# Moving the keys' sine products from GpSimd to VectorE in the first attention layer

## The reference, cut to what matters

```python
def _rotate_half(x):
    half = x.shape[-1] // 2
    return jnp.concatenate([-x[..., half:], x[..., :half]], axis=-1)
...
kv_r = kv_c * cos + _rotate_half(kv_c) * sin
scores = jnp.einsum('bhsr,bhlr->bhsl', q_r, k_r)
attn = jax.nn.softmax(scores, axis=-1)
ctx_c = jnp.einsum('bhsl,bld->bhsd', attn, kv_r)
```

## Time and profile before

| | |
|---|---|
| device time, median of 3 runs | 3006.91 us (3006.22 to 3009.59) |
| device time of the profiled execution | 3003.31 us |
| its span | 3001.5 us |
| mean granted TensorE clock | 0.958 |
| TensorE busy (matmul) | 2737.8 us, 91% |
| VectorE busy | 1884.5 us, 63% |
| ScalarE busy | 1130.2 us, 38% |
| GpSimd busy | 1837.4 us, 61% |

### The profile page before, as it was taken

One profiled execution on the slowest core, in us unless ns is written; L12 is line 12 of the kernel. 1 busy time (PEld: TensorE's weight loads), 2 busy tenths in 40 slices (PEclk: granted clock), 3 DMA queues, 4 the chain that ended last, 5 costly groups with the idle time before them and its releaser, 6 DMA issues. The chain is left out here.

```text
span 3001.5 us, 43374 instructions
## 1 busy us (share of the span) xinstructions
PE 2737.8 (91%) x16024; PEld 1697.7 (57%) x16024; DVE 1884.5 (63%) x2324; ACT 1130.2 (38%) x1641; POOL 1837.4 (61%) x1233
## 2 busy tenths in 40 slices
PE   7689999999999998998789979999999999997998
PEld 6445554555555454554678865555555555555665
DVE  3486666665766576663666656765765765675664
ACT  2124441444134432443333224443443443442331
POOL 0369985999669975994200008877877877950111
PEclk8689999999999999998899989999999999998998
DMA  9323341333213431333000042332333323301000
GB/s 302 107 75 94 78 117 32 76 89 93 70 46 93 100 88 32 80 83 110 1 1 1 1 86 65 88 80 67 87 72 74 84 66 81 89 9 49 7 7 13
DMA packets 98842, 209.21 MB, mean 70 GB/s; under 512 B 30306, under 2 KB 74322, under 8 KB 91116
## 3 DMA queue, kind: packets, MB, share of 16 engines
q1 hardware_dynamic: 98636, 206.44, 26.8%
HBM read 135.36 MB, written 46.00 MB: 60 GB/s over the span
## 5 line engine op out<-in xcount | busy, mean ns | idle before, releaser
L1423 DVE TENSOR_REDUCE maxpart<-pair 112x2 f32<-112x1000 f32 x748 | 896.2, 1198 | 461.8 <-PE pair L1055 460.1
L1242 ACT ACTIVATE prob<-wide 125x896 f32<-125x896 f32 x768 | 675.0, 917 | 809.1 <-PE wide L1081 556.6
L1309 POOL TENSOR_TENSOR sums<-sums,prob 125x448 f32<-125x448 f32 x544 | 675.7, 1263 | 47.8 <-POOL sums L1309 39.3
L1312 POOL TENSOR_TENSOR sums<-sums,prob 125x896 f32<-125x896 f32 x284 | 615.0, 2166 | 117.5 <-ACT prob L1242 81.2
L1095 PE MATMUL single<-prob,kv 125*64 125x448 f32 x3072 | 672.0, 551 | 0.7 <-ACT prob L1242 0.7
L1076 PE MATMUL wide<-qhigh,kparts 64*125 64x448 f32 x3072 | 451.4, 371 | 14.0 <-ACT prob L1242 12.4
L1055 PE MATMUL pair<-kparts,qhigh 64*112 64x500 f32 x1496 | 337.1, 446 | 61.4 <-DVE maxpart L1423 53.5
L1095 PEld LDWEIGHTS single<-prob,kv 125*64 125x64 f32 x3072 | 211.5, 136 | 253.4 <-issue 190.4
L1055 PEld LDWEIGHTS pair<-kparts,qhigh 64*112 64x112 f32 x1496 | 131.0, 171 | 361.8 <-DVE maxpart L1423 190.3
L1076 PEld LDWEIGHTS wide<-qhigh,kparts 64*125 64x125 f32 x3072 | 282.1, 184 | 84.8 <-issue 30.4
L1081 PE MATMUL wide<-shift,ones_row 64*125 64x448 f32 x1536 | 283.9, 364 | 0.2 <-DMA shift<-maxrow 0.2
(11 more groups left out here) (406 smaller groups left out, 4034.4 us busy)
## 6 DMA issues: line engine op xcount, KB each, us to landing
kparts<-keys_merged SPq DMA_DIRECT2D x64, 750.0 KB, 8.9
kparts<-kparts SPq DMA_DIRECT2D x96, 250.0 KB, 3.1
keys_merged<-kparts SPq DMA_DIRECT2D x32, 750.0 KB, 10.4
recip<-zrec_merged SPq DMA_DIRECT2D x124, 112.0 KB, 2.8
w_low_values<-w_merged SPq DMA_DIRECT2D x64, 192.0 KB, 2.8
raw<-in_ctx SPq DMA_DIRECT2D x32, 375.0 KB
values_merged<-kv SPq DMA_DIRECT2D x32, 375.0 KB
kv<-values_merged SPq DMA_DIRECT2D x32, 375.0 KB
```

The source lines that it names most:

```text
L1242: nc.scalar.activation(prob[:, n_ % NPROB, :].rearrange("p (a b) -> p a b", a=2), acc[0:LP, :, 0:HQ], ACT.Exp)\
L1309: nc.gpsimd.tensor_tensor(dst[:, cols], first_in[:, cols], prob[:, n_ % NPROB, cols], ALU.add)\
L1312: nc.gpsimd.tensor_tensor(dst, first_in, prob[:, n_ % NPROB, :], ALU.add).then_inc(s["pool_sum"], 1)
L1423: V.tensor_reduce(maxpart[:, b % 2, t:NMAX:4, third], acc[0:TQ, :, 0:LB], AX.X, ALU.max).then_inc(*R.signal_drained(kind, *key))
```

## The change

From batch 3 on, the step `rotate` on GpSimd is gone from the list. In its place VectorE has two steps `sine`, one for each half of the features, with the same operands, shape and count of `rope_sin`. While batch `b` is at pair 2 the first is issued for batch `b + 3`; at pair 4 the second, followed by the first half of the cosine products, which stood at pair 3; the second half of the cosine products, which stood at pair 4, moves to pair 0 of the next batch. `rope` stays at pair 1. Batches 0 to 2 keep their rotation on GpSimd. All products read `raw` and a table and write to SBUF.

```diff
@@ -310,8 +310,6 @@
                 ahead(t + 1)
                 if j + 1 < BG and p == 4:
                     add("maxT", b + 1, region=3)
-                if p == 3 and b + 3 < NB:
-                    add("rotate", b + 3)
                 if p in (2, 3) and b + 2 < NB:
                     add("keyT", b + 2, p - 2, region=3)
                 if p == 5 and j < BG - 1 and b + 2 < NB:
@@ -329,8 +327,13 @@
                     if b + 2 < NB:
                         add("rope", b + 2, 0)
                         add("rope", b + 2, 1)
-                if p in (3, 4) and b + 3 < NB:
-                    add("ropecos", b + 3, p - 3)
+                if p == 2 and b + 3 < NB:
+                    add("sine", b + 3, 0)
+                if p == 4 and b + 3 < NB:
+                    add("sine", b + 3, 1)
+                    add("ropecos", b + 3, 0)
+                if p == 0 and 1 <= b and b + 2 < NB:
+                    add("ropecos", b + 2, 1)
                 if p == 4 and j == BG - 1 and b + 2 < NB:
                     add("keyT", b + 2, 2, region=3)
                 if p == 5 and b + 2 < NB:
@@ -1336,6 +1339,12 @@
                         dve.wait_ge(s["tables_loaded"], 32)
                     dve.wait_ge(s[f"ctx_loaded_{b % 2}"], 16 * (b // 2 + 1))
                     V.tensor_tensor(rope_c[:, tiles, :], raw[:, b % 2, tiles, :], cosk[:, tiles, :], ALU.mult).then_inc(s["rope_cos"], 1)
+                elif kind == "sine":
+                    b, part = key
+                    dve.wait_ge(s["rope_done"], 2 * b)
+                    dve.wait_ge(s[f"ctx_loaded_{b % 2}"], 16 * (b // 2 + 1))
+                    own, other = (slice(0, DC // 2), slice(DC // 2, DC))[::1 - 2 * part]
+                    V.tensor_tensor(rope_s[:, :, own], raw[:, b % 2, :, other], sink[:, :, own], ALU.mult).then_inc(s["rope_sin"], 1)
                 elif kind == "rope":
                     b, part = key
                     tiles = slice(part * LT // 2, (part + 1) * LT // 2)
```

## The result

| | before | changed |
|---|---|---|
| device time, median of 4 runs | 3006.56 us | 2963.40 us (2962.20 to 2970.34) |
| ratio, with its 95% interval | | 0.9862 [0.9846, 0.9877] |
| profiled execution: device time, span | 3003.31, 3001.5 us | 2962.20, 2960.4 us |

The kernel became faster by 1.4%, 43 us in the medians and 41.1 in the profiled spans.

What follows compares the result with a forecast made beforehand. GpSimd was taken to pace the first layer's full stretches. Removal 1.75 us less, added product costs 1.0 more: 0.75 less a stretch; 14.3 and 1.2 make 15.5 off 3006.9, so 2991.4 us, range 2974 to 3012.

Steps and rivals of the forecast that it cites:

- GpSimd paces the full stretch, TensorE's floor is 26.65: First layer: GpSimd's work sets the 29.70 us between context copies; TensorE's limit allows at most 3.05 us gain.
- The removal, 1.75 us a stretch: Two sine products leave GpSimd at pair 3: 1.92 us out, a 0.17 us wait in, 1.75 us less.
- VectorE has room, and the context rows come in time: VectorE, 18.88 of 29.70 us busy, takes 1.1 more; context rows, wanted 1.4 us earlier, add nothing.
- (1) The first sine product at 298.5 is 0.76 into the pair of 297.74: 0.76 + 0.55 - 0.12 = 1.2: At pair 2, VectorE's first sine product lengthens GpSimd's pair of half sums by 1.2 us.
- The rule behind it: A VectorE product costs GpSimd its own length, plus how far into a half sum it starts, less 0.12 us.
- (2) ... 1.55: At pair 4, the second sine and first cosine product, 1.02 us together, cost GpSimd's half sums 1.55 us.
- (3) and (4): At pair 0, cosine plus context product cost GpSimd 1.1 us; at pair 1, the rotation's sums cost 1.2.
- The weighing of the rule of the Trainium skill: Shared port: the trace agreed on which instructions collide, not who waits; a product seemed to start within a running half sum.
- The stretches: First layer: 15 full and four second-batch stretches gain 0.75 us each, 14.3; three seventh-batch ones half, 1.2 us.
- The whole: Whole kernel: 15.5 us less, from 3006.9 to 2991.4 us.
- Rival (b): Sine products on VectorE cost GpSimd nothing and TensorE becomes the bound: 46 us less, 2961 us; chance 0.08.
- the forecast 1.0: Extra cost to GpSimd's half sums per full stretch from products on VectorE: 5.05 us against 4.07 before.

## Why the prediction was wrong, step by step

- **GpSimd paces the full stretch, TensorE's floor is 26.65:** right. The changed kernel is still paced by GpSimd, and the stretch without rotation stayed at 26.63.
- **The removal, 1.75 us a stretch:** right; 1.88 alone.
- **VectorE has room, and the context rows come in time:** right. Its products took 0.55, the first 0.81, and no maximum was late by more than a tenth.
- **"(1) The first sine product at 298.5 is 0.76 into the pair of 297.74: 0.76 + 0.55 - 0.12 = 1.2":** this is the step that failed. 0.31 was measured. The rule behind it was read from four meetings, three of which followed a maximum; the fourth, behind a key remainder, had cost 0.37, and it fitted only because its place happened to be near 0. In all four the half sum that was stretched had begun after the instruction in front of the product; here the running one had begun 0.14 before the key remainder, and the product did not cut in but waited, and cost less than its own length. This term is 0.9 of the missing 1.2 us.
- **"(2) ... 1.55":** 1.25, as the row came 0.39 and not 0.65 into its half sum: the shifts that (1) set off were wrong with it. **(3) and (4),** 1.1 and 1.2: 1.03 and 1.29, right.
- **The weighing of the rule of the Trainium skill** ("SBUF — State Buffer", section "Who interferes with whom") came out too hard on it. The product that seemed to begin within a running half sum had the port already: that half sum's record runs from 305.76, but it was held until the product's end. Where VectorE has not claimed ahead, its product does wait until the half sum is over, as the Trainium skill has it (0.81, and up to 1.57 in the runs). That section speaks of who issues first; that VectorE holds the port while the instruction in front of its product still runs, it does not say.
- **The stretches:** the three at the seventh batch were counted for half of 0.75 and gave 3.1, 2.4 and 0.8; the four at the second batch gave 1.5 each. At the seventh batches a term was missing, TensorE's clock: before, all three ran at a granted clock of 0.95 with TensorE busy 28.9 to 29.0 us; in the changed kernel the first two ran at 1.00 with 27.08, the third at 0.95 with 28.69. In the third, TensorE was busy 0.67 us from 1008 to 1011 and was then granted 0.50, the lower of its two levels (1.2 GHz), from 1012 to 1014; in the first, busy 0.32 us from 390 to 392, it kept 1.00. So the third gained least because its clock still fell.
- **The whole:** of the 27.7 us between forecast and result, 16.5 are the full stretches (1.85 instead of 0.75), 3.1 the second batches, 5.0 the seventh, 1.0 the rest of the span, and 2.1 come from medians that fell more than the profiled spans.
- **Rival (b)** named 2961, two us from the result, by another way: its mark, ScalarE no longer waiting for the sums, did not come. The products are not free: between the run with the cosine products moved alone and the changed kernel the stretch fell by 0.6 and not by 1.75, so they cost 1.15.

In short: what paces the stage and the price of the removal were right. The rule for what a product costs GpSimd was wrong: VectorE does not cut into a running half sum, but holds the next one ahead of its product, or waits. That the added products cost nearly the forecast 1.0 (0.93 with the cosines left, 1.15 with them moved) was luck of the sum. What was missed is that the order on VectorE changes the price of all meetings. The cosine products' new places alone gave 20 of the 43 us, and the prediction had treated them as a detail of the walk.

## What to carry to other kernels

Where VectorE and GpSimd both work from SBUF, look at the instruction in front of each VectorE product with two SBUF inputs. In these traces, a GpSimd instruction that began within a long one lost the product's length and the time that the long one still ran (1.25 us at 301.04); one that had begun before the instruction in front lost less than the product's length (0.31), and VectorE waited; a row of three products claimed once lost GpSimd 1.18. A move of work between engines and a move of other work within one engine, in the same change, are priced separately: here each was worth about the same. Taking a claim away helps the engine that was held and makes the other late: here it paid in the kernel before (0.7 to 0.8%) and not in the changed one.

## What was not expected of the hardware

- VectorE holds the shared port before its product begins: one memset of 0.06 us between a maximum and a product takes 2.6 us a stretch off GpSimd's busy time (26.27 to 23.69) and lets the same product take up to 1.57 us instead of 0.62.
- A row of products that was claimed ahead runs through with GpSimd held (three products in 1.48 us); a row that was not lets a half sum in between each two, so that the second takes 1.5 us. What decides it in the queue is not shown by these runs.
- Behind a key remainder a claim can be lost: 24 half sums that began 0.10 to 0.28 us into one ended 1.0 after it and made the product wait 1.45 us, 47 that began 0.40 us or more into one were held to the product's end.
- A half sum held to a product's end ends 1.0 us after it in every meeting looked at, as before the change.
